# Attention on one core: products for maxima issued one by one around the score products, transposed maxima kept in the scores' PSUM and copied by ScalarE

## What is computed

```python
def _L0_xattn_ref(Q, K, V, attention_mask, w_q, w_k, w_v, w_o, b_o):
    q = (Q @ w_q.T).reshape(B, S, G, HG, HD)      # G = 8 groups, HG = 4 heads each, HD = 16
    k = (K @ w_k.T).reshape(B, S, G, HD)
    v = (V @ w_v.T).reshape(B, S, G, HD)
    scores = jnp.einsum('bnghd,bmgd->bnghm', q, k) / scale
    scores = jnp.where(pad, NEG_INF, scores)
    scores = jnp.where(causal, scores, NEG_INF)
    attn = jax.nn.softmax(scores, axis=-1)
    out = jnp.einsum('bnghm,bmgd->bnghd', attn, v).reshape(B, S, D)
    return out @ w_o.T + b_o
...
x = x + jnp.tanh(g_xattn[0]) * _L0_xattn_ref(_layernorm(x, axis=-1), ctx_2048, ctx_2048, ...)
x = x + jnp.tanh(g_ffn[0]) * _L0_ffn_ref(_layernorm(x, axis=-1), ...)
```

## Time and profile before

| | |
|---|---|
| median of three runs | 1355.91 us (1350.62 to 1359.08) |
| profiled execution: its time | 1353.09 us |
| its span, first to last instruction | 1351.3 us |
| PE busy with matmuls, weight loads | 94%, 69% |
| DVE, ACT, POOL busy | 48%, 43%, 48% |
| granted TensorE clock, mean | 0.979 |
| max products, first and last start | 93.5 and 405.8 us |
| score products, first and last start | 123.1 and 420.5 us |

### The profile page before, as it was taken

One profiled execution on the slowest core, in us unless ns is written; L12 is line 12 of the kernel. 1 busy time (PEld: TensorE's weight loads), 2 busy tenths in 40 slices (PEclk: granted clock), 3 DMA queues, 4 the chain that ended last, 5 costly groups with the idle time before them and its releaser, 6 DMA issues. The chain is left out here.

```text
span 1351.3 us, 27369 instructions
## 1 busy us (share of the span) xinstructions
PE 1272.3 (94%) x8553; PEld 936.9 (69%) x8554; DVE 646.7 (48%) x1861; ACT 586.4 (43%) x1016; POOL 642.8 (48%) x722
## 2 busy tenths in 40 slices
PE   8998999999997998999999799999999999999995
PEld 5554544444443357778767589999989988889894
DVE  4345788888896654686304113232343333333300
ACT  1222566666663223222222145555545444445452
POOL 6000333333332431443455266666666666666664
PEclk8999999999998997999999899999999999999998
DMA  9452333333343404000013225555555554665433
GB/s 338 150 162 89 111 109 100 97 107 99 95 126 120 159 1 187 32 32 32 32 55 103 96 52 139 141 142 142 137 132 141 142 139 129 157 174 129 91 71 39
DMA packets 73615, 152.94 MB, mean 113 GB/s; under 512 B 10725, under 2 KB 16357, under 8 KB 72793
## 3 DMA queue, kind: packets, MB, share of 16 engines
q1 hardware_dynamic: 52104, 100.27, 22.1%
q0 software_dynamic: 21456, 51.97, 18.4%
HBM read 97.56 MB, written 52.23 MB: 111 GB/s over the span
## 5 line engine op out<-in xcount | busy, mean ns | idle before, releaser
L202 DVE CUSTOM_DVE_ANT_0 a_mb<-a_mb,late 128x128 f32<-128x128 f32 (+3 forms) x512 | 244.4, 510 | 50.8 <-PE a_mb L183 44.1
L1439 DVE CAST e_w<-e_w 128x480 fp32r<-128x480 f32 x135 | 75.5, 568 | 360.4 <-DMA e_w<-in_w2T 360.4
L634 ACT ACTIVATE a_at<-a_eb 128x1024 f32<-128x1024 f32 (+3 forms) x256 | 179.6, 705 | 102.4 <-PE a_eb L696 101.8
L570 POOL TENSOR_SCALAR_AFFINE_SELECT a_at<-a_at 128x256 f32<-128x256 f32 x256 | 105.5, 412 | 225.4 <-ACT a_at L634 225.2
L1593 PE MATMUL e_yps<-e_w,e_hT 128*128 x711 | 197.3, 404 | 0.9 <-ACT e_hT L1504 0.9
L1572 PE MATMUL e_gate<-e_w,e_xT 128*128 x948 | 169.8, 328 | 8.5 <-DVE e_w L1448 7.8
L1572 PEld LDWEIGHTS e_gate<-e_w,e_xT 128*128 128x128 f32 x948 | 156.7, 190 | 20.7 <-issue 16.4
L1572 PE MATMUL e_up<-e_w,e_xT 128*128 x948 | 170.6, 329 | 0.0
L1572 PEld LDWEIGHTS e_up<-e_w,e_xT 128*128 128x128 f32 x948 | 149.8, 188 | 0.0
L1593 PEld LDWEIGHTS e_yps<-e_w,e_hT 128*128 128x128 f32 x711 | 128.1, 189 | 25.5 <-issue 1.2
L1470 POOL TENSOR_TENSOR e_hT<-e_hc,e_hT 128x384 fp32r<-128x384 f32 x79 | 84.3, 1067 | 118.9 <-ACT e_hc L1505 118.9
(11 more groups left out here) (235 smaller groups left out, 1844.5 us busy)
## 6 DMA issues: line engine op xcount, KB each, us to landing
e_w<-in_w13T SPq DMA_DIRECT2D x16, 1408.0 KB
dq<-p_parts SPq DMA_DIRECT2D x32, 256.0 KB, 2.4
a_q<-dq SPq DMA_DIRECT2D x64, 128.0 KB
do<-a_o SPq DMA_DIRECT2D x32, 256.0 KB, 2.1
e_w<-in_w2T SPq DMA_DIRECT2D x16, 512.0 KB
a_k<-dk SPq DMA_DIRECT2D x64, 98.0 KB
e_w<-in_ctxT SPq DMA_DIRECT2D x4, 1024.0 KB, 13.9
e_w<-in_x SPq DMA_DIRECT2D x4, 1024.0 KB, 13.2
```

What stands on the lines that cost most here:

```text
L202: eng.tensor_tensor_reduce(out=b[:, 0:w], in0=b[:, 0:w], in1=io["late"][:, SEQ - w:SEQ], scale=1.0, scalar=3 * NEG, op0=ALU.add, op1=ALU.m ...
L570: eng.affine_select(out=square, in_=square, compare_op=ALU.is_ge, fill=0.0, base=0, pattern=[[0, 2], [1, P]], channel_multiplier=-1).then_ ...
L634: eng.activation(at[r % 2][:, ch, 2 * hp:2 * hp + 2, ch * P:SEQ], eb[hp][:, :, ch * P:SEQ], ACT.Exp, scale=0.25).then_inc(s_exp, 1)
```

## The change

Three things are changed. (1) Max products are issued singly by find_maxima, each with a wait of its own. A step u now has product 2u+1 first, then the two score products with the half that the max product did not use ahead (argument order), then product 2u+2, then the value products. Product 0 of a round stands at the end of step 7 of the round before it (first_maxima), and the wait for its loaded q and k moves there too. (2) The ring holds no transposed maxima any more. Its two skipped places are spread, one ahead of product 4 and one ahead of product 12 (SLOTS, PERIOD, free). A product waits for the reduction of the product three before it, but 4, 5, 12 and 13 wait for that of the product two before. (3) The transpose stands in step 2, between the first max product and the score products, and writes into columns 0 to 127 of a_eb0, which the score products of piece 1 leave alone; ScalarE copies it to a_mrow ahead of its exponential of that step, where VectorE did before.

```diff
+SLOTS = [m + (m >= NOPS // 4) + (m >= 3 * NOPS // 4) for m in range(NOPS)]
+PERIOD = NOPS + 2
...
+def free(m):
+
+    slot = SLOTS[m] - RING
+    while slot % PERIOD not in SLOTS:
+        slot -= RING
+    return SLOTS.index(slot % PERIOD) + slot // PERIOD * NOPS + 1
+
+
+def find_maxima(eng, io, i, r, m):
+
+    t, j, ch = OPS[m]
+    if not isinstance(i, int) or i * NOPS + free(m) > 0:
+        eng.wait_ge(io["s_rmax"], i * NOPS + free(m) + 1)
+    rows, w = slice(HALF * t, HALF * t + ROW_MAX), max(256, (ch + 1) * P)
+    eng.matmul(bank(io, m)[:, 0:w], io["q"][r][rows, j, ch * P:(ch + 1) * P], io["k"][r][rows, 0:w],
+               start=True, stop=True).then_inc(io["s_smax"], 1)
...
+        turned = eb[0][0:HG * CH, 1, 0:P]
...
+            def take_row(i, r, t):
+                if after(i, 1):
+                    eng.wait_ge(s_row[(r - 1) % NB], ROWS * (t + (r - 1) // NB + 1))
+                eng.wait_ge(io["s_mt"], i + 3)
+                eng.activation(io["mrow"][(r + 1) % 2], turned, ACT.Copy).then_inc(s_mr, 1)
+
...
                         eng.wait_ge(s_sexp, e + 2)
+                        if ch == 1 and hp == 0 and exists(i + 1):
+                            take_row(i, r, t)
...
-                        take_row(eng, io, i + 1, r + 1)
...
-            def exp_unit(i, r, ch, j):
+            def exp_unit(i, r, ch, j, order):
...
+                if ch == 1 and j == 0 and exists(i + 1):
+                    turn_maxima(eng, io, turned, r + 1, (i + AHEAD) * NOPS + 1)
-                for t in range(2):
+                for t in order:
...
                 for ch in range(CH):
                     for j in range(2):
+                        m = 2 * (2 * ch + j) + 1
                         if exists(i + AHEAD):
-                            max_pair(eng, io, i + AHEAD, (r + AHEAD) % NB, ch, j)
-                        exp_unit(i, r, ch, j)
+                            find_maxima(eng, io, i + AHEAD, (r + AHEAD) % NB, m)
+                        exp_unit(i, r, ch, j, (1 - OPS[m][0], OPS[m][0]))
+                        if m + 1 < NOPS and exists(i + AHEAD):
+                            find_maxima(eng, io, i + AHEAD, (r + AHEAD) % NB, m + 1)
+                        elif m + 1 == NOPS and exists(i + AHEAD + 1):
+                            first_maxima(i + AHEAD + 1, (r + AHEAD + 1) % NB, t + (r + AHEAD + 1) // NB)
                         pv_units(i, r, 2 * ch + j)
-                    if ch == 0 and exists(i + 1):
-                        turn_maxima(eng, io, r + 1, (i + AHEAD) * CH * HG + HG if exists(i + AHEAD) else NIT * CH * HG + 1)
```

More of the change, by code:

```diff
@@ L155, in load_values @@
     eng.dma_start(io["v"][r][:], io["v_all"][:, bass.ds(i, 1)].rearrange("p i j w -> p (i j) w")).then_inc(io["s_v"][r], 16)
[L158 to L184, removed]
@@ L187, in turn_maxima @@
-def turn_maxima(eng, io, r, done):
-    eng.wait_ge(io["s_rmax"], done)
[L190 to L203, removed]
@@ new lines, in turn_maxima, with take_maxima @@
+def turn_maxima(eng, io, turned, r, done):
+    eng.wait_ge(io["s_rmax"], done)
+    eng.transpose(turned, io["mx"][r % 2].rearrange("p h c -> p (h c)"), io["ident"]).then_inc(io["s_mt"], 1)
+def take_maxima(eng, io, i, r, m, due=None):
+    t, j, ch = OPS[m]
+    h, b, w = 2 * t + j, bank(io, m), (ch + 1) * P
+    if isinstance(i, int):
+        eng.wait_ge(io["s_smax"], i * NOPS + m + 2)
+    else:
+        eng.wait_ge(io["s_smax"], eng.snap(due))
+        eng.reg_add(due, due, 1)
+    eng.tensor_tensor_reduce(out=b[:, 0:w], in0=b[:, 0:w], in1=io["late"][:, SEQ - w:SEQ], scale=1.0, scalar=3 * NEG,
+                             op0=ALU.add, op1=ALU.max, accum_out=io["mx"][r % 2][:, h, ch:ch + 1]).then_inc(io["s_rmax"], 1)
@@ L466, in scores @@
             def scores(n):
-                round, turn, j = n // (2 * CH), n // 2 % CH, n % 2
                 if n == 0:
                     eng.wait_ge(s_vcp, BATCH + 1)
[L470 to L474, removed]
+                for at in range(2 * n, 2 * n + 2):
+                    round, m = divmod(at, NOPS)
+                    if m == 0:
+                        eng.wait_ge(io["s_ld"][round], LD)
+                    find_maxima(eng, io, round, round, m)
+                if 2 * n == NOPS + 2:
+                    eng.wait_ge(s_klo, BATCH + 1)
+                    turn_maxima(eng, io, proj[KD][0:HG * CH, 0:P], 0, NOPS + 1)
             def queries(b):
@@ L645, in body @@
             def body(i, r, t):
[L646 to L653 removed]
+                if exists(i + AHEAD):
+                    for m in range(NOPS):
+                        take_maxima(eng, io, i + AHEAD, r, m, due)
             steps(eng, body)
```

34 lines of the change are left out of this document (15 added, 19 removed).

## The result

The changed kernel takes 1493.78 us in the median of four executions (1490.75 to 1495.83), the kernel before 1354.45 in four beside it. The ratio is 1.1025, with a 95% interval of 1.0984 to 1.1067: slower by 139 us where 1369 was forecast, and outside the range. The profiled execution took 1490.75, with a span of 1489.0 against 1351.3. In the executions of both kernels, and in the experiments, the time goes with the granted clock, so each is given with its mean clock.

A forecast was written before the change was run, and what follows sets the result against it. Bound by a latency circle through PE and DVE; 24 rounds at 0.49 us give 11.8, plus 1.5 to 2 for six others, total +13.5 on 1355.9: 1369 us, range 1353 to 1382.

The forecast's parts named there:

- The walk: Attention round of the new queue priced load by load from product 1: 9.74 us against 9.25, so 0.49 longer.
- The wait of product 13 for reduction 11: Step 5: product 13 waits for a 512-wide reduction two before it; 1.48 us from product 11, adding 0.5.
- what steps 1 and 2 lose: Transpose inside step 2 makes steps 0 to 2 together 4.24 us instead of 4.01.
- The rounds that are written out: Six attention rounds outside the loop: 1.5 to 2 us added for all together.
- ScalarE's copy at nothing: Copy of the 16x128 row, about 0.28 us per round on ScalarE, hidden by slack; costed at nothing.
- The wait for the loads at its earlier place: Wait for loaded q and k, one set of value products earlier at a round's end; delays nothing.
- The cast at nothing: Removed VectorE cast of 0.28 us per round; falls beside a gap, worth at most 0.28, counted as nothing.
- The transpose among half-row products: Step 2: transpose pays two more drains; the lower bound, no extra cost, is 0.2 less per round, 1363 us.
- A: Reductions run free and PE alone sets a round: 8.55 us, 0.70 less than 9.25; 1335 us, chance 0.12.
- C: Weight load of the second max product exposed at four more places: 0.44 us per round, 1381 us; chance 0.15.
- B: Gains cancel losses, leaving only product 13's wait: about 0.1 us per round, 1356 to 1359 us; chance 0.18.
- D: No effect in the loop, as both versions wait for something else such as ACT's chain: 1356 us; chance 0.03.

The follow-up runs named there:

- experiment 2: Kernel before plus two 128x512 copies on VectorE behind each round's cast, TensorE's order untouched; 1491.49 and 1430.45 us.
- experiment 10: Kernel before plus a 128x8 copy on VectorE behind each pair of reductions; seven of nine executions 1355.78 to 1363.7 us, others 1374.56 and 1467.13.
- eleventh experiment: Kernel before plus a 128x64 copy on VectorE behind each pair of reductions; 1441.26 and 1406.8 us.
- 3: Changed kernel plus five filler matmuls of 128 columns, results unread, ahead of product 13; 1378.48 us, ratio 1.0169.
- 7: Kernel before plus two 128x512 VectorE copies per round and eight filler matmuls ahead of the max pair 6 and 7; 1370.62 us, ratio 1.0114.
- Experiment 1: Changed kernel with the ring's two skipped slots ahead of products 6 and 7 instead of 4 and 12; 1351.13 us, ratio 0.9979.
- experiment 5: Changed kernel with the transpose moved ahead of product 5, behind value products; 1484.9, 1490.29, 1480.33 and 1430.22 us.
- experiment 6: Changed kernel plus two filler matmuls ahead of product 13; 1370.03, 1373.82, 1430.34 and 1497.83 us.
- experiment 4: Kernel before, pairs kept, with only the transpose into the scores' PSUM and ScalarE's copy replacing VectorE's cast; 1358.3 us, ratio 1.0013.
- 9: Kernel of Experiment 1 plus a 16x128 copy on VectorE behind reduction 3; 1350.69 us, ratio 0.9988 against the kernel before.
- experiment 8: Changed kernel with free slots ahead of products 6 and 7 and the transpose ahead of product 5; 1356.63 us, ratio 1.0016.

## Why the prediction was wrong

**The step that failed** is in the prediction's first paragraph: "The clock is 1.00 and the DMA share 0.32, so neither clock nor transfers matter." The first half of the sentence was a reading, and the second didn't follow from it. A clock of 1.00 is what the order of before earned. The walk then added 0.49 us to each round in which PE does the same work and so idles longer, and never asked whether the clock would hold. It didn't: it fell to 0.50 in round 9, and a round at that clock takes 14.72 where one at full clock takes 9.62. None of the rivals has it, and this is why the range could miss by over 100 us. What I took as a cost of 13 us was also the cause of one of about 125. That PE's longer waits take the clock is shown by experiment 2 (added waits alone lose it) and by 10 and 11 (0.22 us more a round lost it once clearly in nine executions, 0.25 in both), and 3 and 7 show that work put ahead of the wait keeps it.

**The walk itself held.** A round of the changed kernel at 2.4 GHz was to be 9.74, or 9.20 + 0.49 = 9.69 by difference, and is 9.62. Five of six distances are within 0.05. The wait of product 13 for reduction 11 is there as worked out, 1.47 with 0.52 of idle time put down to DVE (in round 8 it lies 0.50 ahead of product 12 and 0.21 ahead of 13). Experiment 1, which moves the free slots, takes 0.25 off this step and 0.26 off the one in which product 4 waits, and in all 0.44 off a round. The prediction had put what steps 1 and 2 lose down to the transpose alone; product 4's wait is as much a part of it, as experiments 1 and 5 show, where the move of either gives it back. With the clock kept, in experiment 6, the program takes 1370 to 1374. By my estimate the fillers' 0.22 in each of 24 rounds are 5 of that, so the change alone would be at 1365 to 1369, beside a forecast of 1369.

**The smaller terms.** The rounds that are written out, at 1.5 to 2 us for six: too low; from transpose to transpose the first three take 9.29, 9.28 and 9.42 against 8.82, 8.82 and 8.74, together 1.6 more. ScalarE's copy at nothing: right (experiment 4, 1.0013). The wait for the loads at its earlier place at nothing: not tried alone, but the distance from product 13 to the next 1, which holds it, is 1.96 where the walk without it had 2.01. The cast at nothing: right (9). The transpose among half-row products at 0.2 a round above the lower bound: right in size (0.18 by experiment 5), but only with those slots; in experiment 8 it is nothing.

**The rivals.** A, reductions run free: false, product 13 waits as priced. C, a second weight load that is exposed: false; product 7 to 9, with product 8 between, takes 1.01, where an exposed load would make it 1.13. B and D would need rounds of 9.2 to 9.3 at full clock, and they are 9.62. Without the fall of the clock the forecast's mechanism would have stood; with it, the time was missed by 125 us. The assumption that I called the weakest, the latency of a product that comes alone, was sound: 0.60 for 384 columns and 0.66 for 512, where the walk had 0.61 and 0.66.

## What to carry to other kernels

Before pricing an order of PE's queue in terms of waits, add up what PE leaves idle in a round before and after; if a change adds to it in a stage that runs at 2.4 GHz for long, the loss of the clock is a rival with its own price, here 5.1 us on a round of 9.6, ten times the wait that caused it. Take the sum from the products' own time and the length of the round, not from PE's busy share. It gives a warning and not a limit, since it doesn't order all kernels here. Where such a wait can't be avoided, products that nobody reads, put into it, can hold the clock for a fraction of the loss (0.4 against 5.1 us a round), but a better place for the free buffers is cheaper: one line gave back all 139 us.

## What the runs showed of the hardware

The fall needs little. No weight load in the changed kernel's rounds of the loop at full clock waited over 0.53 us, and 0.22 us more per round brought the kernel before to the edge. I had thought of the clock as something that a kernel loses by long stalls. The Trainium skill, page "TensorE: Matmul & The Clock Gate", section HAM oscillation, describes its loss where PE waits long for transfers, again and again. This case's trace goes further than that case of the page: the waits here are for VectorE and 0.2 to 0.53 us long, and in this order they are enough.

The clock doesn't come back by itself within the stage. At 0.50 the rounds leave PE hardly idle, and yet it stays there for 345 us: PE is busy for 99.23 of 100 us in the changed kernel, and for 99.86 in experiment 2, whose pairs leave gaps in the record at full clock (91.89 in the kernel before). In the eleventh experiment it stays for all 19 rounds that are left. Why the clock doesn't return at such a busy share is open. What would bring it back inside the stage wasn't tried.

At the edge one program takes very different times: 1370 or 1498 in experiment 6, 1356 or 1467 in experiment 10. Such a spread is a sign of this edge.

PE's busy share depends on the form of the products more than on the work. From 300 to 400 us PE is busy for 99.89 us in the kernel of experiment 1 and for 91.89 in the kernel before, with rounds of 9.18 and 9.24 and the same products:

```profile
300.00:400.00 100.00, 99.89 (x1151) 58.21 (x1152) 88.02 (x352) 68.41 (x110) 35.94 (x88) 1.00 0.36 107
```
```profile
300.00:400.00 100.00, 91.89 (x1145) 43.28 (x1147) 89.80 (x361) 65.97 (x99) 35.43 (x88) 1.00 0.36 105
```

The first is experiment 1, the second the kernel before.

A reduction that comes 0.3 to 0.35 late appears in one or two rounds between 175 and 205 us of several kernels (0.95 behind the load of product 7 in the changed kernel, the fifth reduction in experiment 9, a step of 1.25 in place of 0.96 in experiment 10). It is not in the profiled execution of the kernel before. Since the changed kernel and the fifth experiment lost their clock in such a round, it may have set the moment of the fall; experiments 1, 3, 9 and 10 had it and kept the clock, so it isn't enough. Its cause is open.

The kernels of experiments 1 and 9 are the fastest that ran, 0.2% and 0.1% below the one before, and neither interval excludes 1. So the parts of the change, at their best, make a kernel that is as fast as the one before, and not one that is faster.
